# Reordering an attention kernel on one core: a tile's statistics, the weighed values, the third tile and the last step

## What is computed

```
cq  = rms(xn @ Wq_down) * q_norm          # 192 wide
ckv = rms(xn @ Wkv_down) * kv_norm        # 128 wide
kpe = rope(rms(xn @ Wk_pe) * k_pe_norm)   # 64 wide, one for all heads
q   = [cq @ Wq_up, rope(cq @ Wq_pe)]      # 16 heads of 128 + 64
k,v = ckv @ Wkv_up                        # 8 heads of 128, each used by two query heads
y   = softmax(causal(q @ [k, kpe]^T / sqrt(192))) @ v
out = x + (y @ Wo) + ternary(xn) @ (ternary(weight) + rram_variation)^T
```

## Time and profile before

| | us |
|---|---|
| median of three runs (1780.68 to 1782.37) | 1781.77 |
| the profiled execution, its own time | 1778.57 |
| its span, first to last instruction | 1776.8 |
| PE busy in it | 1694.7 (95%) |
| DVE busy | 1318.8 (74%) |
| ACT busy | 1135.2 (64%) |
| mean granted TensorE clock | 0.989 of full |

### The profile page before, as it was taken

The page is one execution under the profiler, slowest core; times in us unless marked ns, Lnnn a source line. Parts: engine busy times, 40 slices in busy tenths (PEclk is TensorE's granted clock), DMA queues, the critical chain, the costliest instruction groups (busy, mean ns, idle before and its releaser), DMA issues.

```text
span 1776.8 us, 29329 instructions
## 1 busy us (share of the span) xinstructions
PE 1694.7 (95%) x9200; PEld 851.4 (48%) x9200; DVE 1318.8 (74%) x3368; ACT 1135.2 (64%) x2463; POOL 592.9 (33%) x1042
## 2 busy tenths in 40 slices
PE   4579999999999999999999999999999999999998
PEld 4345545444544545544454445554454454544443
DVE  5678777777778777777777777876877877777673
ACT  6566666656667566666757566665766666665663
POOL 1223333333333333333433333334333433333231
PEclk8899999999999999999999999999999999999999
DMA  9337877878868877886869978786886888897775
GB/s 281 71 62 127 151 141 148 150 139 144 152 118 153 158 142 150 151 155 112 159 125 162 171 133 148 141 150 125 150 158 130 161 134 148 150 158 139 147 141 107
DMA packets 911733, 255.05 MB, mean 144 GB/s; under 512 B 897368, under 2 KB 899674, under 8 KB 911194
## 3 DMA queue, kind: packets, MB, share of 16 engines
q1 hardware_dynamic: 902336, 235.29, 74.5%
q10 hardware_dynamic: 8794, 15.80, 2.8%
q0 software_dynamic: 448, 2.10, 0.4%
HBM read 20.32 MB, written 8.39 MB: 16 GB/s over the span
## 4 chain that ended last, share of the span: by engine, by line
PE 80%; DVE 8%; ACT 5%; issue 4%; DMA 2%; SPq 1%; ACTq 0%; POOL 0%; DVEq 0%; POOLq 0%
PE bank L569 6%; PE bank L570 6%; PE bank L572 6%; PE bank L571 6%; PE bank L602 6%; PE bank L603 6%; PE bank L604 6%; PE bank L620 5%; PE bank L622 5%; PE bank L621 5%; PE bank L581 3%; DVE F L1285 2%; DVE P L1271 2%; DMA XT<-XS 2%; PE bank L574 2%
## 5 line engine op out<-in xcount | busy, mean ns | idle before, releaser
L880 ACT ACTIVATE P<-P,nm 128x512 f32<-128x512 f32 (+7 forms) x512 | 394.9, 772 | 405.6 <-DVE nm L1271 403.9
L1271 DVE CUSTOM_DVE_ANT_0 P<-bank,mask,neg 128x512 f32<-128x512 f32 (+7 forms) x512 | 402.4, 815 | 246.3 <-PE bank L581 126.9
L1464 POOL TENSOR_SCALAR sn<-sm 128x1 f32<-128x1 f32 x512 | 239.5, 468 | 1000.4 <-ACT P L880 990.3
L875 ACT ACTIVATE F<-P,rc 128x512 f16<-128x512 f32 (+7 forms) x512 | 368.2, 765 | 164.2 <-DVE rc L1279 162.4
L1285 DVE SCALAR_TENSOR_TENSOR F<-P,rc,F 128x512 f16<-128x512 f32 (+7 forms) x512 | 404.6, 811 | 0.0
L569 PE MATMUL bank<-K,Q 128*128 128x512 f16 (+3 forms) x760 | 248.6, 327 | 6.3 <-DMA Q<-QS 6.0
L570 PE MATMUL bank<-K,Q 128*128 128x512 f16 (+3 forms) x760 | 248.7, 327 | 0.0
L572 PE MATMUL bank<-K,Q 128*128 128x512 f16 (+3 forms) x760 | 248.7, 327 | 0.0
L571 PE MATMUL bank<-K,Q 128*128 128x512 f16 (+3 forms) x760 | 248.7, 327 | 0.0
L602 PE MATMUL bank<-FT,V 128*128 128x512 f16 x576 | 220.3, 382 | 7.5 <-DMA FT<-F 5.9
L603 PE MATMUL bank<-FT,V 128*128 128x512 f16 x576 | 219.3, 381 | 0.0
(11 more groups left out here) (203 smaller groups left out, 2629.1 us busy)
## 6 DMA issues: line engine op xcount, KB each, us to landing
out<-X ACTq DMA_DIRECT2D x32, 256.0 KB, 3.4
X<-in_x ACTq DMA_DIRECT2D x28, 256.0 KB, 3.7
FT<-F SPq DMA_TRANSPOSE x352, 4.3
wo<-in_Wo SPq DMA_DIRECT2D x4, 1024.0 KB, 8.6
V<-CC SPq DMA_DIRECT2D x32, 64.0 KB, 2.0
Q<-QS SPq DMA_TRANSPOSE x128, 4.0
X<-in_x SPq DMA_DIRECT2D x4, 256.0 KB, 7.6
ua<-in_Wq_up SPq DMA_DIRECT2D x1, 1024.0 KB, 7.2
```

The source lines that it names most:

```text
L875: return e.eng.activation(dst, src, ACT.Copy, scale=scale)
L880: e.eng.activation(m.P[:, u % 4, 0:w], m.P[:, u % 4, 0:w], ACT.Exp, bias=m.nm[:, u % 8:u % 8 + 1], scale=-1.0, accum_out=m.sm[:, u % 8:u % ...
L1271: e.eng.tensor_tensor_reduce(out=m.P[:, u % 4, 0:w], in0=m.pS[u % 2][:, off:off + w], in1=m.mask[:, 1024 - w:1024], scale=m.neg[:, :], sca ...
```

## The change

It moves work in the order of the engines; except at the very end no instruction is added or dropped.

1. **Statistics.** `stats` of a tile (DVE) moves from (g, p) = (0, 1) to (3, 1) of the step before, with that of tile 3 inside the prologue's loop at u = 3. For this `load_x` moves from (3, 1) to (2, 1) and `store_out` from (2, 1) to (1, 1).
2. **Weighed values.** `values_hi(n)` (ACT) moves from the head of step n + 1 to the end of step n, between the two `scaled_hi` of half 1. `values_lo(n - 1)` (DVE) now precedes the maxima also at g = 1. In wide steps `inverse` stands earlier, around the first `scaled_lo`.
3. **Third tile.** The work of tile 2 listed above moves into steps 0 to 3, where the later tiles have it.
4. **Last step.** PE leaves out the interleaved `combine` of the last steps: after `weigh(126, ...)` come `combine(125)`, `weigh_pair(127, 0)`, `weigh_pair(127, 1)`, `combine(126)`, `combine(127)`. `weigh_pair` waits for the FT of its two heads only and has 256 columns a matmul. `accumulate` and `store_out` of the last tile are done in two halves of 256 columns. DVE does the last two `scaled_lo` before `values_lo(125)`.

```diff
@@ tensor_attention @@
+    def weigh_pair(n, p):
+        b, i, g = where(n)
+        for u in (4 * n + 2 * p, 4 * n + 2 * p + 1):
+            z = GROUP_OF[u]
+            e.wait_ge(s.ft_in[z % FSLOTS], 16 * (z // FSLOTS + 1))
+        if p == 0:
+            e.wait_ge(s.yl, n - 1)
...
+        for j in range(i + 1):
+            V = m.V[:, key_slot(b, j), :, :]
+            e.eng.matmul(o, V[:, 0, :], ft[:, :, j, :], start=(j == 0), stop=False)
+            e.eng.matmul(o, V[:, 0, :], ft[:, :, i + 1 + j, :], start=False, stop=False)
+            op = e.eng.matmul(o, V[:, 1, :], ft[:, :, j, :], start=False, stop=(j == i))
+            if p:
+                op.then_inc(s.pv, 1)
...
-                e.wait_ge(s.od, 3)
+                e.wait_ge(s.cr, 3)
...
-    e.wait_ge(s.cr, 3)
-    tiles.ffn(2, m.pO)
-    for n in range(N):
+    for n in range(N - 1):
...
-            if q == 1 and (g == 3 and t + LEAD < T or g == 0 and t and t + LEAD - 1 < T):
+            if q == 1 and (g == 3 and t + LEAD < T or g == 0 and t + LEAD - 1 < T):
...
-            if q % 2 and n:
+            if q % 2 and n and n + AHEAD < N:
                 combine(n - 1, q // 2)
-    combine(N - 1, 0)
-    combine(N - 1, 1)
+    for n in (N - 3, N - 2, N - 1):
+        combine(n, 0)
+        combine(n, 1)
+        if n == N - 3:
+            weigh_pair(N - 1, 0)
+            weigh_pair(N - 1, 1)
@@ scalar_attention @@
-    tiles.parts_hi(2)
...
-            if p == 0 and n:
-                values_hi(n - 1)
...
-            elif t and t + LEAD - 1 < T and (g, p) == (0, 1):
+            elif t + LEAD - 1 < T and (g, p) == (0, 1):
                 tiles.parts_hi(t + LEAD - 1)
...
             if u < 4 * N:
                 scaled_hi(u)
+            if u == 4 * N - 2:
                 scaled_hi(u + 1)
-            if (g, p) == (2, 1) and t:
+            if p:
+                values_hi(n)
+            if u < 4 * N - 2:
+                scaled_hi(u + 1)
+            if (g, p) == (1, 1) and t:
                 store_out(t - 1)
-            if (g, p) == (3, 1) and t + LEAD + 1 < T:
+            if (g, p) == (2, 1) and t + LEAD + 1 < T:
                 load_x(t + LEAD + 1)
-    values_hi(N - 1)
-    store_out(T - 1)
+    store_half(0)
+    store_half(1)
@@ vector_attention @@
+        if u == 3:
+            tiles.stats(3)
...
-    tiles.ffn_out(2, m.pO)
-    tiles.parts_lo(2)
...
+        first = wide or g == 1
...
+            if u == 4 * N:
+                scaled_lo(u - 2)
+                scaled_lo(u - 1)
-            if p == 0 and n and wide:
+            if p == 0 and n and first:
                 values_lo(n - 1)
             if u < 4 * N:
                 maximum(u)
                 maximum(u + 1)
-            if p == 0 and n and not wide:
+            if p == 0 and n and not first:
                 values_lo(n - 1)
...
-            if u <= 4 * N:
+            if u < 4 * N:
                 scaled_lo(u - 2)
+            if wide:
+                inverse(u)
+            if u == 4 * N - 2:
+                inverse(u + 1)
             if p == 0 and n + 2 * AHEAD < N:
                 queries.rotate(n + 2 * AHEAD)
-            if u <= 4 * N:
+            if u < 4 * N:
                 scaled_lo(u - 1)
-            if u < 4 * N:
-                inverse(u)
-                inverse(u + 1)
+                if not wide:
+                    inverse(u)
+                if u < 4 * N - 2:
+                    inverse(u + 1)
...
-            if t + LEAD < T and (g, p) == (0, 1):
-                tiles.stats(t + LEAD)
+            if t + LEAD + 1 < T and (g, p) == (3, 1):
+                tiles.stats(t + LEAD + 1)
...
-    accumulate(T - 1)
+    accumulate_half(0)
+    accumulate_half(1)
@@ gpsimd_attention, sync_attention @@
-    tiles.rotate_keys(2)
-    tiles.keys(2)
-    tiles.keep(2)
...
```

More of the change, by code:

```diff
@@ L604, in weigh @@
         e.eng.matmul(o, V[:, 1, :], hi, start=False, stop=(j == i)).then_inc(s.pv, 1)
+    def weigh_pair(n, p):
[5 more added lines that the diff above has]
+            e.wait_ge(s.yl, n - 1)
+        at = FT_AT[n] * 1024
+        ft = m.FT[:, at:at + 1024 * (i + 1)].rearrange("p (h c q) -> p h c q", h=4, q=128)[:, 2 * p:2 * p + 2, :, :]
+        o = m.pY[n % 2].rearrange("p (h q) -> p h q", h=4)[:, 2 * p:2 * p + 2, :]
+        for j in range(i + 1):
[5 more added lines that the diff above has]
+                op.then_inc(s.pv, 1)
     def combine(n, p):
@@ L907, in store_out, with store_half @@
         e.eng.dma_start(rows(out, t), m.X[:, t % XSLOTS, :]).then_inc(s.st_o, 16)
+    def store_half(k):
+        e.wait_ge(s.acc, T + k)
+        if k == 0:
+            e.wait_ge(s.st_o, 16 * (T - 1))
+        at = slice(256 * k, 256 * k + 256)
+        e.eng.dma_start(rows(out, T - 1)[:, at], m.X[:, (T - 1) % XSLOTS, at]).then_inc(s.st_o, 16)
     def outputs_out(o):
@@ L955, in scalar_attention @@
                 scaled_hi(u)
+            if u == 4 * N - 2:
                 scaled_hi(u + 1)
-            if (g, p) == (2, 1) and t:
+            if p:
[3 more added lines that the diff above has]
+            if (g, p) == (1, 1) and t:
                 store_out(t - 1)
-            if (g, p) == (3, 1) and t + LEAD + 1 < T:
+            if (g, p) == (2, 1) and t + LEAD + 1 < T:
                 load_x(t + LEAD + 1)
-    values_hi(N - 1)
-    store_out(T - 1)
-    e.wait_ge(s.st_o, 16 * T)
+    store_half(0)
+    store_half(1)
+    e.wait_ge(s.st_o, 16 * (T + 1))
 class VectorTiles:
@@ L1299, in accumulate, with accumulate_half @@
                                    op0=ALU.mult, op1=ALU.add).then_inc(s.acc, 1)
+    def accumulate_half(k):
+        X = m.X[:, (T - 1) % XSLOTS, 256 * k:256 * k + 256]
+        e.wait_ge(s.c, N)
+        e.wait_ge(s.od, T)
+        e.eng.scalar_tensor_tensor(out=X, in0=m.pO[:, 256 * k:256 * k + 256], scalar=m.invo[:, :], in1=X,
+                                   op0=ALU.mult, op1=ALU.add).then_inc(s.acc, 1)
     def outputs_lo(o):
@@ L1341, in vector_attention @@
                 maximum(u + 1)
-            if p == 0 and n and not wide:
+            if p == 0 and n and not first:
                 values_lo(n - 1)
-            if t and t + LEAD - 1 < T and (g, p) == (0, 1):
+            if t + LEAD - 1 < T and (g, p) == (0, 1):
                 tiles.ffn_out(t + LEAD - 1, m.pY[(n + 1) % 2])
-            if u <= 4 * N:
+            if u < 4 * N:
                 scaled_lo(u - 2)
+            if wide:
+                inverse(u)
+            if u == 4 * N - 2:
+                inverse(u + 1)
             if p == 0 and n + 2 * AHEAD < N:
                 queries.rotate(n + 2 * AHEAD)
-            if u <= 4 * N:
+            if u < 4 * N:
                 scaled_lo(u - 1)
-            if u < 4 * N:
-                inverse(u)
-                inverse(u + 1)
+                if not wide:
+                    inverse(u)
+                if u < 4 * N - 2:
+                    inverse(u + 1)
             if p and n + 2 * AHEAD < N:
@@ L1482, in gpsimd_attention @@
                     queries.rotated_lo(n + 2 * AHEAD)
-            if t and t + LEAD - 1 < T:
+            if t + LEAD - 1 < T:
                 if (g, p) == (1, 0):
@@ L1619, in sync_attention @@
                 tiles.turn_x(t + LEAD)
-            if (g, p) == (2, 0) and t and t + LEAD - 1 < T:
+            if (g, p) == (2, 0) and t + LEAD - 1 < T:
                 tiles.keep(t + LEAD - 1)
```

## The result

| us | before | after |
|---|---|---|
| median of the runs | 1781.8 (4 runs, 1780.7 to 1782.4) | 1771.7 (4 runs, 1767.9 to 1773.2) |
| profiled execution, its span | 1778.57, 1776.8 | 1767.90, 1766.1 |

The ratio is 0.9941, 95% interval 0.9924 to 0.9958: faster, by 10 us where 27.2 were forecast, and outside the range (1748.5 to 1764). A second set of five runs gave 1771.2. The runs of the kernel after lie 5 us apart, those of before under 2.

The account below looks back on a forecast made before the run. PE's own work was taken as the bound, so only its idle or half-clock time could be won. 13.5 + 2.1 + 6.1 + 5.5 = 27.2 us off the median 1781.77 gave 1754.6, range 1748.5 to 1764.

Parts of the forecast that it names:

- (c): store_out and load_x a step sooner: booked 0, nearest a step's middle with free DMA; nothing to 1.3 us each.
- I leave them as they are: PE's other waits, for FT and XT (4.4 us), hang on the transposes: left unchanged, bounds 4.4 us gain or loss.
- Waits for YL: Short tiles: earlier YL and YH remove PE's waits, 13.5 us over three patterns, plus 2.1 in the first tiles.
- (a): On ACT, values_hi(n) inside step n waits for weigh(n) and delays scaled_hi(u + 1): cost 0, at most 0.6 us.
- (b): On DVE, statistics at (3, 1) put 0.8 us ahead of the next step's YL: cost 0, at most 0.8 us.
- Part 3: Steps 0 and 1: first combine at 117.9 instead of 122.96, 6.1 us gained, with clock loss before weigh(0) booked.
- Part 4: The end: combine(127) ends at 1768.0 instead of 1773.5, 5.5 us gained, with 2.3 us idle and the clock kept.
- B: Waits move on: PE meets FT, XT or later YL; half of 15.6 us and 2.5 come back, 1765; chance 0.22.
- D: Slower: loads and stores sent a step sooner hold up the transposes at (1, 1) and (2, 1), 1796; chance 0.03.

Follow-up runs that it names:

- e_late: The changed kernel with store_out and load_x a step later again, at their old places, and a sixth slot of X: 1754.4 us.
- u_stats: e_late with the statistics at (0, 1) again, and so five slots of X: 1764.5 us.
- l_values: e_late with values_hi at the head of the next step again: 1758.7 us.
- c_fill_swap: e_late with ffn(2) back before weigh(0), and SP sending the FT of half 0 ahead of the queries: 1856.1 us.

## Why the prediction was wrong, point by point

- **The step that failed is part 1 and 2's (c)**: "their total does not change; what they meet does ... nearest is the middle of a step with free DMA, so 0". The cost lies within the bounds, nothing to 1.3 us at each transfer; the choice between them was made without looking where (1, 1) and (2, 1) fall. Taking the move away gives 1754.4 us for 1771.7: the term is 17.3 us (16.3 by the gains), 0.54 a tile, and sits at the last steps of the long tiles, about 1.5 us at each. The bounds knew only the time of the bytes; the larger part, 0.8 us a place, is that SP takes longer to send its transposes beside the early store, so that all that stands behind them is late. The trace of before held half of what was needed: the engines are full there (share 1.13 from 366 to 378) and PE already waited 0.43 us for FT.
- **"I leave them as they are", for the waits of FT and XT**, bounds 4.4 us either way, failed with it. The waits went from 4.4 to 15.6 us. The bound was taken from waits that were there, when the size of the next one is set by how late SP sends, how long the transpose flies and when PE comes for it. With the transfers late, the sum rose only to 6.6 us in `e_late`, inside the bounds.
- **Waits for YL**: right. 15.6 us were forecast for the short tiles with the first; `e_late` against the kernel before gains 15.1 us between `combine(8, 0)` and `combine(104, 0)` and 2.0 from `combine(3, 0)` to `combine(8, 0)`. The change kept 2.9 of the former. (a) and (b), both booked at 0: no wait took their place. `u_stats` shows the move of the statistics to be worth 5.7 us and more, `l_values` that of `values_hi` perhaps 2.
- **Part 3**: 6.1 forecast. In this execution WO came 2.2 us later; the matmuls were already 2.4 us late at 66 us, ahead of anything the edit touches, and the input loads took longer to land. Counted from there, the first `combine` starts at 118.3 for 117.9 forecast, but the second at 126.3 for 124.6, since YL was late once more (0.69 and 1.30 us, forecast as none). That leaves 4.4 us by the trace; undoing it costs 5.3 by the medians. The clock fell before `weigh(0)` as booked, at a larger price: 0.60 over 4 us is 1.6 us, not 0.6.
- **Part 4**: 5.5 forecast; 5.1 by the traces, 4.0 by the medians. The one wait for FT is 2.45 us for 2.3 forecast. That the clock was kept in this trace is luck: it was booked because 2.3 is nearer to 1.90 than to 3.48, but with the same ending it fell in seven of eleven traces.
- **The sum** of 27.2 is near for the kernel without the early transfers (26.4 us under the kernel before on the same chip), in part by luck: by the traces the tiles gave 17.1 for 15.6, part 3 4.4 for 6.1. Undone one at a time, its parts give 10.0 (statistics), 4.3, 5.3 and 4.0, or 23.6, by the medians, and 11.5, 5.8, 6.8 and 3.3, or 27.4, by the gains.
- **The rivals.** B had the waits for FT right, but not their cause: without the early transfers PE, free of YL, meets only 2.2 us more of FT and XT (6.6 for 4.4), and the size of 10.3 came from halving. D named the mechanism, loads and stores that hold up the transposes, and its deciding point, 0.85 us a tile, was not reached: 0.54. It was given a chance of 0.03 because it was put only as the case in which the change is slower; its weaker form, which eats part of the gain, was in no case. The Trainium skill, "DMA: Bandwidth & Descriptors", under "Issuing engines are not separate DMA queues", has transfers of all engines interleave on the same 16: the traces agree, in the longer flights above and in the XT that took 3.6 us longer to land behind a store and a load.

What stays open: why sending a transpose from SP takes longer beside a store from ACT; why PE waited 0.4 us longer for the last FT in the change than in `e_late`; how much of `u_stats`' 10 us is more than the 5.7 and the clock; and whether the half-clock stretches explain the whole spread of the change's runs, as one execution of each kernel has a trace, and two of the change.

## What to carry to other kernels

When a load or store is moved, even by half a step, look at the DMA share of the stretch where it will land, at the transposes in flight there, and at how long the other queue takes to send its own. A page's median of landing times hides this; the waits of the engine that is the bound do not. When a wait is taken from the bounding engine, work out how much time is left to each transfer that it meets next, and give a case to each mechanism in the size in which it eats part of the gain, not only in the one in which it turns the sign.

## What the runs showed of the hardware

**Here a store on one queue slowed the sending on another.** Beside the store from ACT, an instruction of SP that sends a transpose took 3.10 us instead of 2.10, and the four ahead of the last FT 0.8 us more on average (8.8 to 8.9 for 7.8 to 8.1 us), in all five traces that have the store there.

**The clock.** Its fall does not follow from the length of the gap alone. In the second profile of the change (stretches, columns as above) a gap of 2.05 us at 371.6 lost the clock and one of 3.61 us at 887.7 kept it:

```profile
371.60:373.60 2.00, 0.00 (x0) 0.00 (x1) 1.29 (x6) 1.07 (x5) 0.42 (x2) 1.00 1.00 208
373.70:375.70 2.00, 2.00 (x6) 0.69 (x6) 0.00 (x0) 0.00 (x0) 0.00 (x0) 0.59 1.33 158
...
887.70:891.30 3.60, 0.07 (x1) 0.00 (x0) 1.54 (x6) 1.15 (x4) 0.56 (x2) 1.00 1.21 187
891.40:893.40 2.00, 2.00 (x12) 1.15 (x13) 0.00 (x0) 0.00 (x0) 0.00 (x0) 1.00 0.91 203
```

From 180 us on, over all traces but `c_fill_swap`, 17 gaps measure 2.0 to 2.7 us: 11 lost the clock and 6 kept it. Gaps of 2.00 and 2.09 us are among those that lost it, gaps of 2.01, 2.09 and 2.45 among those that kept it. One of only 1.46 (in `u_stats`, at 122.5) lost it too. Something besides the length decides; no run here shows what. The prediction's rule, that the nearest known gap decides, has no force between 1.5 and 3.6 us: such a gap is best priced as a chance of some 1.7 us more. The Trainium skill, "TensorE: Matmul & The Clock Gate", under "Why this matters for your kernels", warns of the longer gaps between bursts; these rows agree that gaps cost the clock, but not that their length is enough to tell which.
